# A convolution and whitening kernel: scratch in 4 KB runs, output by whole tiles, and all stores issued by ScalarE

## The chip, the core and the metric

One NeuronCore of a Trainium2 chip runs the whole program. The metric is the device time of one execution in microseconds. Besides the plain times there is one profiled execution, whose trace the rows below come from. The engines are called PE (TensorE, matrix), DVE (VectorE), ACT (ScalarE), POOL (GpSimd) and SP (SyncE, which issues DMAs).

## The reference

Input x is [4, 64, 256, 256] in float32. Layer 0 is a long convolution over both axes with a filter that is separable per channel, plus a bias term; layer 1 whitens the channels:

```python
hx, hy = implicit_filter(z, X...), implicit_filter(z, Y...)   # [256, 64] each: small MLP with sines, times a decay
k = hx[i, c] * hy[m, c]                                        # per channel c, rank one in (i, m)
y = irfft2(rfft2(x, 512) * rfft2(k, 512) / 512)[:256, :256]    # causal 2-D convolution
x = y + x * bias[:, None, None]
x1 = transpose(x, (1, 0, 2, 3)).reshape(64, -1)
x1_s = x1[:, ::9]
cov = x1_s @ x1_s.T / n + 0.01 * eye(64)                       # 64 x 64
deconv = newton_schulz_inverse_sqrt(cov, 5)
out = deconv @ (x1 - mean(x1_s))                               # back to [4, 64, 256, 256]
```

The covariance needs all of the convolved image, so the convolved values have to be kept or stored before the last product can begin.

## The kernel before, in words

**Units.** The convolution is done in 128 units. A unit is one channel of one sweep; a sweep (2 of them) covers two images. Its data are 128 partitions (the row within a half image) by 1,024 floats (image, half, column): 512 KB. Units 0 to 63 are sweep 1, 64 to 127 sweep 2.

**Per unit q.** SP loads x (`load_x`, L204, four units ahead, after `y_done` of the unit that had the slot) and the filter's Hankel block (`load_hankel`, L214, 256 KB in 1 KB runs, three buffers). ACT makes the rounded high parts of the filter, of x and of the middle result V (`flip`, `round_x`, `round_v`), POOL and DVE the low parts. PE makes V (`make_v`) and then y (`make_y`), each from Toeplitz products in three rounded terms and one plain one (L598 to L601; L601 makes two instructions). DVE adds the bias term and writes y to one of two buffers `y_sb` (`finish_y`, L477); for that it waits until the store of unit q - 2 has landed (`y_stored`). POOL masks every ninth value (L337) and DVE sums (L485) for the covariance. SP stores y to the DRAM scratch `convolved` (`store_y`, L216 to L223) in 512 runs of 1 KB, on the same queue as the loads.

**Order on the queues.** In iteration q SP issues `load_x(q + 4)`, `store_y(q - 1)`, `load_hankel(q + 5)`, `load_kept(q)`, each after its waits. ACT does `round_v(q)`, `round_x(q + 2)`, `flip(q + 2)`. PE does `make_v(q + 1)`, `make_y(q)`.

**Kept tiles.** The second product runs over 64 tiles of 128 partitions (channel and half) by 2,048 floats, 1 MB each, in rows of 8 KB. The first 14 are loaded back from the scratch during sweep 2 (`load_kept`, L230 to L239, from unit 68 on one quarter of a tile in each unit: 56 DMAs of 256 KB); seven more go to buffers that come free at the end of the convolution (L269 to L279).

**Between.** After the last unit come the covariance (L630), the Newton-Schulz iterations (small products and DVE steps, L656 to L673), about 664 to 702 us. DVE finishes the last y in two halves (L509), which wait for `y_stored` of unit 125.

**Tile phase.** For each of 64 tiles PE multiplies by the 128 x 128 matrix (L687); ACT evicts one half (L409) and DVE the other (L578) to one of four output buffers, whose earlier store must have landed. SP loads tile t + 21 when PE is done with tile t, then waits for ACT and DVE (L286, L287) and issues the stores of tile t: two DMAs of 64 partitions, 512 KB each, rows of 8 KB straight into the output's layout (L260 to L265).

Of the kernel before, what the change touches and what calls it, by code (L numbers as in the profile page):

```python
# [43 lines left out]
ZW = 2 * C + 1  # L44
X_SLOTS, T_SLOTS, H_SLOTS = 5, 3, 3

TROWS = 8
TW = TROWS * S
TILES = B * (P // TROWS)
KEPT = 14  # L50
PIECES = 4
O_SLOTS = 4
MASK_COLS = 288


def conv_whiten(nc, x, first, hidden, columns, bias, out):
    g_dram = nc.dram_tensor("filters", [2 * C, GLEN], F32, kind="Internal").ap()
    y_dram = nc.dram_tensor("convolved", [B * HB * C, P * S], F32, kind="Internal").ap()

    with ExitStack() as ctx:  # L60
        def sb(name, shape, dt=F32):
# [96 lines left out]
        def wait(eng, s, value):  # L158
            if value > 0:
                eng.wait_ge(s, value)  # L160
# [27 lines left out]
        @block.sync  # L188
        def _(sp):
            sp.dma_start(first_sb, first).then_inc(params_loaded, 16)  # L190
            sp.dma_start(col[:], columns).then_inc(params_loaded, 16)

            sp.wait_ge(w_zeroed, 1)
            for k in range(2):
                h = slice(k * ORDER, (k + 1) * ORDER)
                sp.dma_start(w_sb[h, :, h], hidden[h, :].rearrange("p (l n) -> p l n", l=3)
                             ).then_inc(params_loaded, 16)

            def load_x(q):
                if q >= UNITS:  # L200
                    return

                wait(sp, y_done, q - X_SLOTS + 1)
                sp.dma_start(x_sb[q % X_SLOTS], x[q]).then_inc(x_loaded[q % X_SLOTS], 16)  # L204

            def load_hankel(q):
                if q >= UNITS:
                    return
                k = q % H_SLOTS

                wait(sp, flipped, q - H_SLOTS + 1)
                wait(sp, t_lo_done, q - H_SLOTS + 1)
                src = bass.AP(tensor=g_dram.tensor, offset=(q % C) * GLEN, ap=[[1, P], [C * GLEN, 2], [1, S]])
                sp.dma_start(hankel[k], src).then_inc(hankel_loaded[k], 16)  # L214

            def store_y(q):  # L216
                if q < 0:
                    return
                k = q % 2
                wait(sp, y_done, q + 1)  # L220
                dst = bass.AP(tensor=y_dram.tensor, offset=(q // C) * BLOCKS * C * P * S + (q % C) * P * S,
                              ap=[[S, P], [C * P * S, BLOCKS], [1, S]])
                sp.dma_start(dst, y_sb[k].rearrange("p (i w) -> p i w", w=S)).then_inc(y_stored[k], 16)  # L223

            def tile_in(t, lo, hi):
                image, rows = t // (P // TROWS), t % (P // TROWS)
                return bass.AP(tensor=y_dram.tensor, offset=image * HB * C * P * S + rows * TW + lo,
                               ap=[[P * S, HB * C], [1, hi - lo]])

            def load_kept(q):  # L230
                n = q - (C + 4)
                if not 0 <= n < KEPT * PIECES:
                    return
                w = TW // PIECES
                lo = n % PIECES * w

                for k in range(2):
                    sp.wait_ge(y_stored[k], 16 * (C // 2))
                sp.dma_start(kept[:, n * w:(n + 1) * w], tile_in(n // PIECES, lo, lo + w)).then_inc(kept_loaded, 16)  # L239

            for q in range(4):
                load_x(q)
            sp.dma_start(bias_sb[:], bias.to_broadcast([P, C])).then_inc(bias_loaded, 16)

            sp.wait_ge(filt_ready, 1)
            sp.dma_start(g_dram, filt).then_inc(filt_stored, 16)
            sp.wait_ge(filt_stored, 16)
            for q in range(5):
                load_hankel(q)

            for q in range(UNITS):
                load_x(q + 4)
                store_y(q - 1)
                load_hankel(q + 5)
                load_kept(q)

            def load_tile(t):
                sp.dma_start(t_in[t % slots], tile_in(t, 0, TW)).then_inc(t_loaded[t % slots], 16)

            def store_tile(t):  # L260
                image, rows, k = t // (P // TROWS), t % (P // TROWS), t % O_SLOTS
                for h in range(HB):
                    dst = bass.AP(tensor=out.tensor, offset=image * C * S * S + h * P * S + rows * TW,
                                  ap=[[S * S, C], [1, TW]])
                    sp.dma_start(dst, t_out[k][h * C:(h + 1) * C, :]).then_inc(t_stored[k], 16)  # L265


            sp.wait_ge(y_mm, UNITS)
            for t in range(KEPT, after_v):  # L269
                load_tile(t)  # L270
            store_y(LAST)
            for t in range(after_v, after_y):
                load_tile(t)
            for k in range(2):
                sp.wait_ge(y_stored[k], 16 * (UNITS // 2))
            sp.wait_ge(masked_done, LAST)
            sp.wait_ge(z_last_done, PER)
            for t in range(after_y, slots):
                load_tile(t)  # L279

            for t in range(TILES):
                if t + slots < TILES:
                    sp.wait_ge(t_mm[1], t + 1)
                    load_tile(t + slots)

                sp.wait_ge(t_act, t + 1)  # L286
                sp.wait_ge(t_dve, t + 1)  # L287
                store_tile(t)
            for k in range(O_SLOTS):
                sp.wait_ge(t_stored[k], 16 * HB * (TILES // O_SLOTS))  # L290

        @block.gpsimd
        def _(pool):
# [57 lines left out]
        @block.scalar  # L351
        def _(act):
            def flip(q):
                if q >= UNITS:
                    return
                k, h = q % T_SLOTS, q % H_SLOTS
                act.wait_ge(hankel_loaded[h], 16 * (q // H_SLOTS + 1))

                wait(act, y_mm, q - T_SLOTS + 1)
                nc.scalar.copy(t_f32[k], hankel[h][:, :, :P - 1:-1])  # L360
                nc.scalar.copy(t_hi[k], hankel[h][:, :, ::-1]).then_inc(flipped, 1)  # L361

            def round_x(q):
                if q >= UNITS:
                    return
                k = q % X_SLOTS
                act.wait_ge(x_loaded[k], 16 * (q // X_SLOTS + 1))

                wait(act, v_mm, q - 1)
                nc.scalar.copy(x_hi[q % 2], row_block(k, 0)).then_inc(x_hi_done, 1)  # L370

            def round_v(q):
                k = q % 2
                wait(act, v_mm, q + 1)

                wait(act, y_mm, q - 1)
                nc.scalar.copy(v_f32[k], ps_v[k][:, :, S:2 * S])  # L377

                nc.scalar.copy(v_hi[k], ps_v[k][:, :, 0:S]).then_inc(v_hi_done, 1)  # L379

            act.wait_ge(rate_ready, 1)
            nc.scalar.activation(decay, pos, ACT.Exp, scale=rate[:]).then_inc(decay_ready, 1)
            round_x(0)
            for layer in range(3):
                act.wait_ge(f_dve, layer + 1)
                nc.scalar.activation(hid, arg, ACT.Sin).then_inc(f_sin, 1)
            round_x(1)
            flip(0)
            flip(1)

            for q in range(UNITS):
                round_v(q)
                round_x(q + 2)
                flip(q + 2)

            act.wait_ge(filt_zeroed, 2)
            nc.scalar.activation(small[:, 7:8], small[:, 7:8], ACT.Sqrt)
            act.wait_ge(n_mm, 1)
            nc.scalar.activation(small[:, 1:2], ps[:, 0, 0:1], ACT.Sqrt).then_inc(n_act, 1)
            act.wait_ge(n_act, 1)  # L400
            nc.scalar.activation(small[:, 3:4], small[:, 1:2], ACT.Sqrt).then_inc(n_act, 1)
            act.wait_ge(d_ready, 1)

            for t in range(TILES):
                act.wait_ge(t_mm[0], t + 1)

                wait(act, t_stored[t % O_SLOTS], 16 * HB * (t // O_SLOTS))
                src = ps[:, bank(t, 0):bank(t, 0) + 2, :].rearrange("p r n -> p (r n)")
                nc.scalar.activation(t_out[t % O_SLOTS][:, 0:TW // 2], src, ACT.Identity,  # L409
                                     bias=small[:, 6:7]).then_inc(t_act, 1)  # L410

        @block.vector
        def _(dve):
# [159 lines left out]
            for t in range(TILES):  # L573
                dve.wait_ge(t_mm[1], t + 1)

                wait(dve, t_stored[t % O_SLOTS], 16 * HB * (t // O_SLOTS))
                src = ps[:, bank(t, 1):bank(t, 1) + 2, :].rearrange("p r n -> p (r n)")
                nc.vector.tensor_scalar(t_out[t % O_SLOTS][:, TW // 2:TW], src, small[:, 6:7], None, ALU.add  # L578
                                        ).then_inc(t_dve, 1)
# [139 lines left out]
```

## Time and profile before

| | us |
|---|---|
| runs of the kernel: median (lowest, highest), 3 runs | 998.5 (994.86, 1002.09) |
| the profiled execution, its own time | 994.94 |
| its span from the first to the last instruction | 993.1 |
| PE busy (matmul) | 881.0 (89%) |
| DVE busy | 574.7 (58%) |
| POOL busy | 496.4 (50%) |
| ACT busy | 397.8 (40%) |
| all DMA, moved | 303.39 MB, mean 306 GB/s |

Busy times are sums over the span, and a busy PE is not a PE at its peak, since matmuls are pipelined. The DMA share is the mean busy share of the core's 16 DMA engines. The convolution takes the span's slices up to about 664 us, the tile phase those from about 702 us.

### The profile page before, as it was taken

How to read it: one execution, taken by the hardware profiler on the slowest of the kernel's cores; microseconds unless marked ns; L12 is line 12 of the kernel's file. 1: busy time of each engine (PE TensorE's matmuls, PEld its weight loads, DVE VectorE, ACT ScalarE, POOL GpSimd, SP SyncE). 2: the span in 40 equal slices, each digit the busy share in tenths (PEclk: the TensorE clock that was granted, in tenths of full speed). 3: DMA queues.
4: the chain of work that ended last, by engine and by line, in shares of the span. 5: the costliest groups of instructions: out<-in, count | busy, mean ns of one | idle time of the engine just before them, and what ended most of it. 6: DMA issues, size and time to landing. Idle time of an engine off the chain costs nothing.

```text
span 993.1 us, 15420 instructions
## 1 busy us (share of the span) xinstructions
PE 881.0 (89%) x5904; PEld 731.0 (74%) x5904; DVE 574.7 (58%) x642; ACT 397.8 (40%) x714; POOL 496.4 (50%) x277
## 2 busy tenths in 40 slices
PE   1799999999999999999999999977997777777896
PEld 0799999999999999999989899976432222222342
DVE  4487788778787657677767676771222222222332
ACT  2455555555555435454444444420121222222332
POOL 2488888889898747777767677760000000000000
PEclk9999999999999999999999999997799999999999
DMA  3799999999999959999999999975499999999999
GB/s 100 161 286 272 275 309 270 268 296 287 282 292 272 298 154 312 320 304 315 309 312 300 296 298 317 312 264 214 142 425 425 427 426 425 426 427 426 362 326 287
DMA packets 147301, 303.39 MB, mean 306 GB/s; under 512 B 10619, under 2 KB 109084, under 8 KB 132636
## 3 DMA queue, kind: packets, MB, share of 16 engines
q1 hardware_dynamic: 147228, 302.41, 92.1%
q8 instruction: 47, 0.77, 0.3%
q14 instruction: 26, 0.21, 0.1%
HBM read 167.96 MB, written 134.41 MB: 304 GB/s over the span
## 4 chain that ended last, share of the span: by engine, by line
PE 47%; DMA 41%; DVE 8%; SPq 2%; issue 1%; ACT 1%; POOL 0%; DVEq 0%; ACTq 0%
DMA convolved<-y_all 24%; DMA out<-z_all 14%; PE ps L601 12%; PE ps L687 10%; PE ps L598 7%; PE ps L599 7%; PE ps L600 7%; DVE y_all L477 4%; PE ps L630 3%; DMA out<-masked_all 2%; DVE z_all L578 1%; SPq L204 1%; ACT z_all L409 1%; DMA plain<-filters 0%; SPq L265 0%
## 5 line engine op out<-in xcount | busy, mean ns | idle before, releaser
L598 PE MATMUL ps<-rounded 128*128 128x256 f32 x1024 | 373.9, 365 | 24.6 <-issue 15.3
L337 POOL TENSOR_TENSOR masked_all<-y_all,mask 128x1024 f32<-128x1024 f32 x127 | 328.8, 2589 | 80.0 <-DVE y_all L477 79.7
L599 PE MATMUL ps<-rounded 128*128 128x256 f32 x1024 | 288.3, 282 | 0.0
L600 PE MATMUL ps<-rounded 128*128 128x256 f32 x1024 | 288.3, 282 | 0.0
L477 DVE SCALAR_TENSOR_TENSOR y_all<-x_all,bias_sb,ps 128x1024 f32<-128x1024 f32 x127 | 162.5, 1280 | 139.9 <-DMA convolved<-y_all 131.7
L598 PEld LDWEIGHTS ps<-rounded 128*128 128x128 f32 x1024 | 197.3, 193 | 30.7 <-issue 30.1
L308 POOL TENSOR_TENSOR rounded<-x_all,rounded 128x512 fp32r<-128x512 f32 x128 | 165.2, 1290 | 88.6 <-ACT rounded L370 87.4
L601 PE MATMUL ps<-plain,x_all 128*128 128x128 f32 x1024 | 197.9, 275 | 0.0
L599 PEld LDWEIGHTS ps<-rounded 128*128 128x128 f32 x1024 | 197.5, 193 | 0.0
L601 PE MATMUL ps<-plain 128*128 128x128 f32 x1024 | 196.7, 274 | 0.0
L600 PEld LDWEIGHTS ps<-rounded 128*128 128x128 f32 x1024 | 193.3, 189 | 0.0
L687 PE MATMUL ps<-kept,z_all 128*128 128x512 f32 x344 | 158.6, 612 | 33.3 <-ACT z_all L409 23.8
L601 PEld LDWEIGHTS ps<-plain,x_all 128*128 128x128 f32 x1024 | 158.2, 191 | 0.0
L687 PEld LDWEIGHTS ps<-kept,z_all 128*128 128x128 f32 x344 | 64.7, 194 | 126.3 <-issue 126.0
L601 PEld LDWEIGHTS ps<-plain 128*128 128x128 f32 x1024 | 157.3, 190 | 0.0
L370 ACT CAST rounded<-x_all 128x512 fp32r<-128x512 f32 x128 | 79.7, 622 | 193.0 <-DMA x_all<-x 193.0
L485 DVE TENSOR_REDUCE z_all<-masked_all 128x116 f32<-128x1044 f32 x127 | 156.7, 1234 | 0.0
L578 DVE TENSOR_SCALAR z_all<-ps,small 128x1024 f32<-128x1024 f32 x48 | 61.6, 1284 | 152.4 <-PE ps L687 94.5
L409 ACT ACTIVATE z_all<-ps,small 128x1024 f32<-128x1024 f32 x48 | 53.5, 1115 | 173.6 <-DMA out<-z_all 124.8
L377 ACT COPY plain<-ps 128x512 f32<-128x512 f32 x128 | 74.8, 584 | 105.5 <-PE ps L601 105.1
L466 DVE TENSOR_TENSOR rounded<-plain,rounded 128x512 fp32r<-128x512 f32 x128 | 93.2, 728 | 8.1 <-ACT rounded L361 8.1
L457 DVE TENSOR_TENSOR rounded<-ps,rounded 128x512 fp32r<-128x512 f32 x128 | 87.2, 681 | 14.0 <-ACT rounded L379 13.9
(98 smaller groups left out, 471.4 us busy)
## 6 DMA issues: line engine op xcount, KB each, us to landing
x_all<-x SPq DMA_DIRECT2D x128, 512.0 KB, 6.9
convolved<-y_all SPq DMA_DIRECT2D x128, 512.0 KB, 8.0
out<-z_all SPq DMA_DIRECT2D x96, 512.0 KB, 12.7
plain<-filters SPq DMA_DIRECT2D x128, 256.0 KB, 9.1
kept<-convolved SPq DMA_DIRECT2D x29, 1024.0 KB, 18.9
out<-masked_all SPq DMA_DIRECT2D x32, 512.0 KB, 12.8
kept<-convolved SPq DMA_DIRECT2D x56, 256.0 KB, 9.5
rounded<-convolved SPq DMA_DIRECT2D x9, 1024.0 KB, 18.8
```

Source lines behind the costliest of these rows:

```text
L308: nc.gpsimd.tensor_tensor(x_lo[k], row_block(q % X_SLOTS, 0), x_hi[k].bitcast(F32), ALU.subtract).then_inc(x_lo_done, 1)
L337: nc.gpsimd.tensor_tensor(masked_of(k, 0, PER), by_image(y_sb[k]), mask_of(q // C, 0, PER), ALU.mult).then_inc(masked_done, 1)
L370: nc.scalar.copy(x_hi[q % 2], row_block(k, 0)).then_inc(x_hi_done, 1)
L457: nc.vector.tensor_tensor(v_lo[k], ps_v[k][:, :, 0:S], v_hi[k].bitcast(F32), ALU.subtract).then_inc(v_lo_done, 1)
L466: nc.vector.tensor_tensor(t_lo[k], hankel[h][:, :, ::-1], t_hi[k].bitcast(F32), ALU.subtract).then_inc(t_lo_done, 1)
L477: nc.vector.scalar_tensor_tensor(y_sb[k], x_sb[q % X_SLOTS], bias_sb[:, q % C:q % C + 1], ps_y[k].rearrange("p a n -> p (a n)"), ALU.mult, ...
L485: nc.vector.tensor_reduce(z_of(q % C), grouped(q % 2, 0, BLOCKS), AX_X, ALU.add).then_inc(z_done, 1)
L598: mm(wide, hi[:, b, cols], t_hi[k][:, f, :], start=True, stop=False)
L599: mm(wide, hi[:, b, cols], t_lo[k][:, f, :], start=False, stop=False)
L600: mm(wide, lo[:, b, cols], t_hi[k][:, f, :], start=False, stop=False)
L601: last = mm(o[:, b, m * S + P:(m + 1) * S], block1[:, b, cols], t_f32[k][:, f, :], start=False, stop=True)
L687: last = mm(ps[:, bank(t, u) + r, :], dmat, t_in[k][:, w:w + IMG], start=True, stop=True)
```

## The change

The scratch gets the layout [sweep x 128, 64 rows x 1,024]: partition (half of the rows, channel), then the row, then image, half and column. A unit's y is stored as 2 x 64 runs of 1,024 floats (4 KB). A tile is now two rows of that layout, still 128 partitions by 2,048 floats, and the kept tiles are loaded in halves, one in every second unit. The output is a tensor of 64 whole tiles, each stored by one DMA of 1 MB; the host puts the axes in order. ACT issues the stores of y (at the end of its iteration, after `flip`) and of the output tiles (after its own half and a wait for DVE's); SP only loads.

```diff
-TROWS = 8
-TW = TROWS * S
-TILES = B * (P // TROWS)
+ROWS = P // 2
+TROWS = 2
+TW = TROWS * XW
+SWEEP_TILES = ROWS // TROWS
+TILES = SWEEPS * SWEEP_TILES
 KEPT = 14
-PIECES = 4
+PIECES = 2
...
-    y_dram = nc.dram_tensor("convolved", [B * HB * C, P * S], F32, kind="Internal").ap()
+    y_dram = nc.dram_tensor("convolved", [SWEEPS * P, ROWS * XW], F32, kind="Internal").ap()
...
-            def store_y(q):
...
-                wait(sp, y_done, q + 1)
-                dst = bass.AP(tensor=y_dram.tensor, offset=(q // C) * BLOCKS * C * P * S + (q % C) * P * S,
-                              ap=[[S, P], [C * P * S, BLOCKS], [1, S]])
-                sp.dma_start(dst, y_sb[k].rearrange("p (i w) -> p i w", w=S)).then_inc(y_stored[k], 16)
...
             def tile_in(t, lo, hi):
-                image, rows = t // (P // TROWS), t % (P // TROWS)
-                return bass.AP(tensor=y_dram.tensor, offset=image * HB * C * P * S + rows * TW + lo,
-                               ap=[[P * S, HB * C], [1, hi - lo]])
+                sweep, rows = t // SWEEP_TILES, t % SWEEP_TILES
+                return bass.AP(tensor=y_dram.tensor, offset=sweep * P * ROWS * XW + rows * TW + lo,
+                               ap=[[ROWS * XW, P], [1, hi - lo]])
 
             def load_kept(q):
-                n = q - (C + 4)
-                if not 0 <= n < KEPT * PIECES:
+                n = (q - (C + 4)) // 2
+                if q % 2 or not 0 <= n < KEPT * PIECES:
                     return
...
             for q in range(UNITS):
                 load_x(q + 4)
-                store_y(q - 1)
                 load_hankel(q + 5)
                 load_kept(q)
...
-            def store_tile(t):
...
-                for h in range(HB):
-                    dst = bass.AP(tensor=out.tensor, offset=image * C * S * S + h * P * S + rows * TW,
-                                  ap=[[S * S, C], [1, TW]])
-                    sp.dma_start(dst, t_out[k][h * C:(h + 1) * C, :]).then_inc(t_stored[k], 16)
...
-            store_y(LAST)
+            sp.wait_ge(y_done, UNITS)
...
-            for t in range(TILES):
-                if t + slots < TILES:
-                    sp.wait_ge(t_mm[1], t + 1)
-                    load_tile(t + slots)
-
-                sp.wait_ge(t_act, t + 1)
-                sp.wait_ge(t_dve, t + 1)
-                store_tile(t)
+            for t in range(TILES - slots):
+                sp.wait_ge(t_mm[1], t + 1)
+                load_tile(t + slots)
...
+            def store_y(q):
+                if q < 0:
+                    return
+                k = q % 2
+                act.wait_ge(y_done, q + 1)
+                dst = bass.AP(tensor=y_dram.tensor, offset=((q // C) * P + q % C) * ROWS * XW,
+                              ap=[[C * ROWS * XW, 2], [XW, ROWS], [1, XW]])
+                act.dma_start(dst, y_sb[k]).then_inc(y_stored[k], 16)
+
             for q in range(UNITS):
                 round_v(q)
                 round_x(q + 2)
                 flip(q + 2)
+                store_y(q - 1)
+            store_y(LAST)
...
                 nc.scalar.activation(t_out[t % O_SLOTS][:, 0:TW // 2], src, ACT.Identity,
                                      bias=small[:, 6:7]).then_inc(t_act, 1)
+                act.wait_ge(t_act, t + 1)
+                act.wait_ge(t_dve, t + 1)
+                act.dma_start(out[t], t_out[t % O_SLOTS]).then_inc(t_stored[t % O_SLOTS], 16)
...
-    out = nc.dram_tensor("out", [B, C, S, S], F32, kind="ExternalOutput").ap()
+    out = nc.dram_tensor("out", [TILES, P, TW], F32, kind="ExternalOutput").ap()
...
+    tiles = r.results[0]["out"].reshape(SWEEPS, SWEEP_TILES, 2, C, TROWS, PER, HB, S)
+
+    return np.ascontiguousarray(tiles.transpose(0, 5, 3, 6, 2, 1, 4, 7)).reshape(B, C, S, S)
```

## Rows read from the trace of the kernel before

**Rows 1.** The page's 40 slices: PE and DMA in tenths busy, GB/s.
```profile
PE   1799999999999999999999999977997777777896
...
DMA  3799999999999959999999999975499999999999
GB/s 100 161 286 272 275 309 270 268 296 287 282 292 272 298 154 312 320 304 315 309 312 300 296 298 317 312 264 214 142 425 425 427 426 425 426 427 426 362 326 287
```

**Rows 2.** The page's chain that ended last: shares by line.
```profile
DMA convolved<-y_all 24%; DMA out<-z_all 14%; PE ps L601 12%; PE ps L687 10%; PE ps L598 7%; PE ps L599 7%; PE ps L600 7%; DVE y_all L477 4%; PE ps L630 3%; DMA out<-masked_all 2%; DVE z_all L578 1%; SPq L204 1%; ACT z_all L409 1%; DMA plain<-filters 0%; SPq L265 0%
```

**Rows 3.** The windows view: busy us (x instructions) by engine, clock, DMA share, GB/s.
```profile
core 0: us, PE busy (x) PEld busy (x) DVE busy (x) ACT busy (x) POOL busy (x), PEclk, DMA share, GB/s
125.00:175.00 50.00, 50.00 (x436) 50.00 (x436) 41.41 (x44) 27.69 (x55) 44.06 (x22) 1.00 0.98 289
425.00:475.00 50.00, 47.33 (x397) 46.10 (x396) 35.60 (x41) 24.31 (x50) 36.03 (x21) 1.00 1.00 311
655.00:702.00 47.00, 33.62 (x209) 30.33 (x210) 18.77 (x42) 2.93 (x6) 8.27 (x8) 0.76 0.53 202
760.00:900.00 140.00, 105.31 (x228) 40.90 (x227) 36.79 (x29) 32.05 (x29) 0.00 (x0) 0.99 1.01 426
```

**Rows 4.** The waits between 380 and 640 us: total us, times, longest.
```profile
ACT rounded L370 <- DMA x_all<-x: 125.2, 51, 4.6
DVE y_all L477 <- DMA convolved<-y_all: 76.3, 51, 3.3
```

**Rows 5.** The DMA view of 5 to 24 us: GB/s in 40 slices.
```profile
GB/s 172 310 311 388 431 414 414 414 414 431 307 115 103 65 4 0 0 0 0 0 0 0 0 0 0 0 0 0 0 0 0 0 0 0 0 0 0 171 243 0
```

**Rows 6.** The DMA view of 80 to 320 us: packets, and the queue's.
```profile
DMA packets 48926, 68.32 MB, mean 285 GB/s; under 512 B 2483, under 2 KB 42252, under 8 KB 48900
...
q1 hardware_dynamic: 48900, 67.96, 96.8%
```

**Rows 7.** The DMA view of 20 to 24 us: packets, and the filter store.
```profile
DMA packets 144, 0.20 MB, mean 49 GB/s; under 512 B 16, under 2 KB 144, under 8 KB 144
...
filters<-kept SPq DMA_DIRECT2D x1, 192.0 KB, 1.9
```

**Rows 8.** The DMA view, issues of the whole span: xcount, KB each, us to landing.
```profile
x_all<-x SPq DMA_DIRECT2D x128, 512.0 KB, 6.9
convolved<-y_all SPq DMA_DIRECT2D x128, 512.0 KB, 8.0
...
kept<-first SPq DMA_DIRECT2D x1, 49.5 KB
...
col<-columns SPq DMA_DIRECT2D x1, 2.0 KB
```

**Rows 9.** The page's packets of the whole span, by size.
```profile
DMA packets 147301, 303.39 MB, mean 306 GB/s; under 512 B 10619, under 2 KB 109084, under 8 KB 132636
```

**Rows 10.** The DMA view of 1.5 to 3 us.
```profile
DMA packets 188, 0.05 MB, mean 35 GB/s; under 512 B 155, under 2 KB 188, under 8 KB 188
```

**Rows 11.** The tile x_all: ns min/median/max, first and last start.
```profile
L477 DVE SCALAR_TENSOR_TENSOR y_all<-x_all,bias_sb,ps x127: 1267/1281/1284, 39.3 to 659.9; 128x1024 f32<-128x1024 f32 x127
...
L509 DVE SCALAR_TENSOR_TENSOR y_all<-x_all,bias_sb,ps x2: 739/742/746, 662.3 to 663.9; 128x512 f32<-128x512 f32 x2
```

**Rows 12.** Line 223: ns min/median/max of the issue, first and last start.
```profile
L223 SPq DMA_DIRECT2D convolved<-y_all x128: 360/434/1462, 41.0 to 665.4; - x128
```

**Rows 13.** SyncE's waits, whole span: total us, times, longest.
```profile
SPq L204 <- DVE y_all L477: 322.1, 122, 16.7
SPq L287 <- DVE z_all L578: 94.1, 43, 3.2
...
SPq L287 <- DVE masked_all L578: 31.9, 14, 3.1
```

**Rows 14.** The chain in order of time: start, us, what.
```profile
929.88 55.19 PE ps L687 x128
```

More of the change, by code:

```diff
@@ L214, in load_hankel @@
                 sp.dma_start(hankel[k], src).then_inc(hankel_loaded[k], 16)
-            def store_y(q):
-                if q < 0:
-                    return
-                k = q % 2
-                wait(sp, y_done, q + 1)
-                dst = bass.AP(tensor=y_dram.tensor, offset=(q // C) * BLOCKS * C * P * S + (q % C) * P * S,
-                              ap=[[S, P], [C * P * S, BLOCKS], [1, S]])
-                sp.dma_start(dst, y_sb[k].rearrange("p (i w) -> p i w", w=S)).then_inc(y_stored[k], 16)
             def tile_in(t, lo, hi):
-                image, rows = t // (P // TROWS), t % (P // TROWS)
-                return bass.AP(tensor=y_dram.tensor, offset=image * HB * C * P * S + rows * TW + lo,
-                               ap=[[P * S, HB * C], [1, hi - lo]])
+                sweep, rows = t // SWEEP_TILES, t % SWEEP_TILES
+                return bass.AP(tensor=y_dram.tensor, offset=sweep * P * ROWS * XW + rows * TW + lo,
+                               ap=[[ROWS * XW, P], [1, hi - lo]])
             def load_kept(q):
-                n = q - (C + 4)
-                if not 0 <= n < KEPT * PIECES:
+                n = (q - (C + 4)) // 2
+                if q % 2 or not 0 <= n < KEPT * PIECES:
                     return
@@ L258, in load_tile @@
                 sp.dma_start(t_in[t % slots], tile_in(t, 0, TW)).then_inc(t_loaded[t % slots], 16)
-            def store_tile(t):
-                image, rows, k = t // (P // TROWS), t % (P // TROWS), t % O_SLOTS
-                for h in range(HB):
-                    dst = bass.AP(tensor=out.tensor, offset=image * C * S * S + h * P * S + rows * TW,
-                                  ap=[[S * S, C], [1, TW]])
-                    sp.dma_start(dst, t_out[k][h * C:(h + 1) * C, :]).then_inc(t_stored[k], 16)
             sp.wait_ge(y_mm, UNITS)
@@ L279, in _ @@
                 load_tile(t)
-            for t in range(TILES):
-                if t + slots < TILES:
-                    sp.wait_ge(t_mm[1], t + 1)
-                    load_tile(t + slots)
-                sp.wait_ge(t_act, t + 1)
-                sp.wait_ge(t_dve, t + 1)
-                store_tile(t)
+            for t in range(TILES - slots):
+                sp.wait_ge(t_mm[1], t + 1)
+                load_tile(t + slots)
             for k in range(O_SLOTS):
-                sp.wait_ge(t_stored[k], 16 * HB * (TILES // O_SLOTS))
+                sp.wait_ge(t_stored[k], 16 * (TILES // O_SLOTS))
         @block.gpsimd
@@ L405, in _ @@
                 act.wait_ge(t_mm[0], t + 1)
-                wait(act, t_stored[t % O_SLOTS], 16 * HB * (t // O_SLOTS))
+                wait(act, t_stored[t % O_SLOTS], 16 * (t // O_SLOTS))
                 src = ps[:, bank(t, 0):bank(t, 0) + 2, :].rearrange("p r n -> p (r n)")
@@ L574, in _ @@
                 dve.wait_ge(t_mm[1], t + 1)
-                wait(dve, t_stored[t % O_SLOTS], 16 * HB * (t // O_SLOTS))
+                wait(dve, t_stored[t % O_SLOTS], 16 * (t // O_SLOTS))
                 src = ps[:, bank(t, 1):bank(t, 1) + 2, :].rearrange("p r n -> p (r n)")
@@ L714 @@
            for k, v in arrays.items()]
-    out = nc.dram_tensor("out", [B, C, S, S], F32, kind="ExternalOutput").ap()
+    out = nc.dram_tensor("out", [TILES, P, TW], F32, kind="ExternalOutput").ap()
     conv_whiten(nc, *aps, out)
     r = run_bass_kernel_spmd(nc, [arrays], core_ids=[0])
-    return r.results[0]["out"]
+    tiles = r.results[0]["out"].reshape(SWEEPS, SWEEP_TILES, 2, C, TROWS, PER, HB, S)
+    return np.ascontiguousarray(tiles.transpose(0, 5, 3, 6, 2, 1, 4, 7)).reshape(B, C, S, S)
```

## The prediction

> **What bounds the kernel now.** I read the page first [rows 1]: PE is busy for nearly the whole convolution (slices up to 655 us), the DMA engines from slice 3 on, and in the tile phase (from 702 us) the transfers stand at 426 GB/s. The chain [rows 2] gives 24% to the stores of y and 16% to the stores of the output. The stretches [rows 3] split the convolution in two. In sweep 1 PE is busy 50.00 of 50 us and issues 436 matmul instructions. Lines 598 to 601 are five instructions (L601 makes two) in each of 8 turns, 40 a unit, so a unit takes 50 x 40 / 436 = 4.59 us, and PE sets it. In sweep 2, with the loads of kept tiles added, there are 397 (PE busy 47.33): 5.04 us a unit, and the waits there [rows 4] name the store of y (76.3 us before L477) and the load of x (125.2 us before L370). So sweep 2 is bound by DMA, 0.45 us a unit over PE.
>
> What a packet costs follows from two windows. Between 5 and 24 us the early loads of x run at 414 GB/s in the steady slices [rows 5], 25.9 GB/s an engine: a 4 KB packet takes 0.158 us. Tiles of 8 KB rows move at 426 GB/s [rows 3], or 0.154 us per 4 KB. In sweep 1 the window 80:320 [rows 6] holds 48,900 packets in 96.8% of 16 engines: 3,717 engine-us. Less the 48,900 - 42,252 = 6,648 packets of 4 KB at 0.158 (1,050) that leaves 2,667 us for 42,252 smaller ones, nearly all of 1 KB: 0.063 us each. Check by sweep 2: per unit and engine 8 x 0.158 (x) + 32 x 0.063 (y) + 16 x 0.063 (hankel) + 8 x 0.08 (kept, half of a 4 KB packet) + 4 closing packets of 0.063 = 5.2 us, against 5.04. The prices hold.
>
> **Part 1, the store of y.** It moves 512 KB as before, now as 128 runs of 4 KB instead of 512 of 1 KB. Spread over 16 engines that is 8 x 0.158 = 1.26 us an engine for 2.02. But is it spread? The destination is now written with 2 (the halves of the partitions) as its outermost size, then 64 rows, then 1,024 elements; it was 128 outermost. The trace tells something of how many engines one DMA gets. Every DMA ends in one small packet per engine: the filter store, of 128 rows, is 144 packets [rows 7]. The whole span has 624 issues (16 lines of that view, from x's 128 to the one of columns, four of them in [rows 8]); with 640 small data packets (128 of columns, 384 of hidden, 128 of bias) and 16 closing ones each that would be 10,624 under 512 B. It has 10,619 [rows 9], five fewer. The window from 1.5 to 3 us shows where: 188 packets, 155 of them small, for the 33 rows of "first" and the 128 of "columns" [rows 10]. 188 - 161 = 27 = 16 + 11: the 33-row transfer ran on 11 engines, the largest divisor of its outer size up to 16. By the same rule the new store, cut along its outer dimension on both sides (2 and 128), runs on 2 engines. The trace can't tell the outer size from the number of runs (both 33 there), and that is the open point. I take the outer size, since a share has to be one stretch of the outer loop of both patterns. All other large DMAs, before and after, have 64 or 128 outermost.
>
> The Trainium skill, "DMA: Bandwidth & Descriptors", section "Why a DMA increments its semaphore by 16 and not by 1", says it outright: the count of engines is the largest up to 16 that divides the outermost non-1 size of both patterns, and on this path it is always the lowest-numbered ones. By that rule the sum below holds; by the number of runs (128, so 16 engines) it would be the first rival. The trace agrees for 33 rows (11 engines); which engines they are, no row shows.
>
> **The sum.** If it is 2 engines, and the same 2 each time, each gets 64 packets of 4 KB a store: 64 x 0.158 = 10.11 us. On them also lie their shares of the loads: x 8 x 0.158 = 1.26, hankel 16 x 0.063 = 1.01, closing packets 0.2: 12.6 us a unit, and 35 us in all for the 14 kept tiles (14 x 8 packets of 8 KB at 0.308). No engine of the core has as much: PE needs 4.59. Two buffers of y keep one store queued behind the other, so these two engines don't idle; DVE's 1.28 us per y [rows 11] lies beside the other store. The last y (units' halves, L509, now at 663.9 us [rows 11]) waits for store 125: first store issued at 41.0 us [rows 12], then 126 x 10.11 = 1,274, loads of the 123 units not yet fetched 123 x 2.27 = 279, closings 25, kept 35: 1,613 us, so 41 + 1,613 + 1.3 = 1,655 against 664: +991. The stores of units 126 and 127 (20 us) and the seven tile loads (7 x 2.46 = 17) then run beside the covariance and the iterations (664 to 702, 38 us): nothing. The profiled execution took 994.94 us (span 993.1, 1.8 outside): 994.9 + 991 = 1,986, say 1,985. The profiled execution lies 0.4% below the runs' median of 998.5, which is nothing beside this.
>
> Bounds of the store's 4 KB packet, which no row shows: below, 0.154 (the tiles' rate, and somewhat less if fourteen engines are out of the way: 0.150); above, 0.168 from the line through 1 KB (0.063) and 8 KB (0.308), and at the far end 4 x 0.063 = 0.252. With 0.150 and a hankel packet at 0.045 (a quarter of 0.154 and a little for the short run): 126 x 9.6 + 123 x 1.92 + 60 = 1,506, in all 1,880. With 0.168: 126 x 10.75 + 123 x 2.35 + 60 = 1,704, in all 2,077; a bubble of 1 us a unit on top, if a full queue holds up the next issue, 2,205. At 0.252: 126 x 16.1 + 123 x 3.0 + 60 = 2,458, in all 2,830, which I hold for unlikely since the load of x has the same runs at 0.158.
>
> **Part 2, who issues.** ACT gets 128 issues of about 0.43 us [rows 12] and waits for the y before each; behind the wait stand the rounding of V and the next flip. ACT is busy 27.7 of 50 us [rows 3], the y is ready 1.3 us after its matmuls while the flip of the same iteration takes about 1.0, and the next V is ready 2.3 us (half a unit of PE) after them: with fast stores no cost, at most 0.43 x 128 = 55 us if nothing hid it; a gain of up to 5 us isn't excluded, as SP's queue gets shorter by these issues. With slow stores ACT is held until y is done, but one unit's V is then rounded already; PE has 12.6 us for 4.59, even at half its clock (9.2), so nothing. SP's wait for y at L204 (322.1 us [rows 13]) stays; what goes is its wait at L287 (94.1 and 31.9 us), behind which the next tile load was queued.
>
> **Part 3, loads of kept tiles**, 28 of 512 KB for 56 of 256 KB: the same bytes, packets of 4 KB for 2 KB, 0. Scratch rows now lie 256 KB apart instead of 128; the output was written at that distance and the tile phase ran at 426 GB/s [rows 3]: 0, bounds -2 and +10.
>
> **Part 4, the tile phase.** 64 stores of 1 MB for 128 of half, contiguous; bytes equal. Loads are released by PE as before, PE by the four output buffers, so loads and stores keep alternating at 426 GB/s until tile 43, and the last 21 tiles go at PE's 3.45 us (16 tiles in 55.19 us [rows 14]). ACT's issue follows DVE's half (1.28 us) and ends before PE's next half: 0, bounds -8 (stores no longer behind loads) and +8. After a slow convolution PE's clock may be low for a while, as between 655 and 702 us (0.76 [rows 3]): up to +10, in the range.
>
> **The rivals.** *All 16 engines take part* (number of runs decides): the y store costs 1.26 us for 2.02, sweep 2 needs 5.2 - 0.76 = 4.4 us of DMA, below PE's 4.59, and its 57 units go from 5.04 to 4.59: -26 us, 969 us: faster. It decides at the engines of a store: with 8 a store would be 16 x 0.158 = 2.53 us on each, more than today's 2.02, so only 16 make it faster. For it: 128 runs, and 33 rows don't exclude it. Against: the only odd transfer followed its outer size. A dearer ACT or tile phase could bring this case to no change. *Two engines, but others each time*: then no engine is overfull, but a store lasts 10.1 us and shares its engines with loads, about 14.3 till it lands; with two buffers a unit takes (14.3 + 1.3 + 1.4) / 2 = 8.5 us: 64 x 3.9 + 62 x 3.46 = +464, 1,460 us. Against it: 11 of 16 in one transfer says nothing of turns, and no row speaks for them. *The change doesn't do what it says* would mean that ACT's stores still wait their turn behind SP's loads; with the larger packets that is about the first rival's time.
>
> **How the numbers follow.** Two fixed engines 0.82, all sixteen 0.15, changing engines 0.03. The two cases of two engines are slower: 0.85. Of the 0.15, 0.12 is faster by over 1% and 0.03 within 1% (1% is about what a measurement of this kernel can tell). The range is the first case's own, 1,830 to 2,240, from 1,880 and 2,205 with some 40 us each way; it leaves out the two rivals and a few hundredths at the edges, 0.2 in all.
>
> **What would show it.** The y store lands 20 us or more after its issue (8.0 now [rows 8]); DMA share in the convolution near (2 x 12.6 + 14 x 2.6) / (16 x 12.6) = 0.3 at 105 to 120 GB/s; PE busy a third or so of each stretch; the chain nearly all convolved<-y_all until 1,650 us; small packets fewer by 14 per y store. The tile phase stays at 426 GB/s and about 290 us. The forecast is wrong if the share stays at 0.9 with units of 4.6 us (first rival), or if stores land in 12 to 15 us with units of 8 (second).

## The result, and the profile after

The changed kernel takes 1,910.6 us (median of 4 runs, 1,909.2 to 1,912.3) against 997.8 before: a ratio of 1.914, 95% interval 1.907 to 1.922. Predicted were 1,985 (1,830 to 2,240), slower. The profiled execution took 1,909.2 us with a span of 1,907.3, against 994.9 and 993.1. All ratios here are of fast executions; one slow one of e6_act_issues (2,482 us) and two of e1_halves (1,006 and 1,008 us) are left out of them, and no trace shows what held them up.

The slices of the page after, under those of [rows 1], with the granted clock:

```profile
PE   4555555555555555665555555555655554977788
...
PEclk9877777777777777787777777777777776999999
DMA  4333333333333333444444444444444432899997
GB/s 130 99 111 111 110 109 111 110 110 110 111 111 110 111 111 110 111 120 130 129 127 118 130 130 128 118 119 129 130 130 127 119 134 103 339 427 427 428 426 309
```

The convolution is stretched to 33 of 40 slices (up to 1,586 us). In it PE is half busy, the DMA engines show a share of 0.3 to 0.4 where they had 0.9, and 99 to 134 GB/s flow where most slices had 264 to 320. The chain by line, against [rows 2]:

```profile
DMA convolved<-y_all 76%; DMA out<-z_all 6%; PE ps L682 5%; DVE y_all L472 4%; DMA out<-masked_all 3%; PE ps L625 1%; DVE z_all L573 0%; ACT z_all L401 0%; DVE masked_all L573 0%; PE ps L596 0%; DVE kept L432 0%; DMA plain<-filters 0%; PE ps L661 0%; PE ps L593 0%; PE ps L665 0%
```

The stores of y have 76% of the span instead of 24%. The stretches that answer to [rows 3] (sweep 1, sweep 2, tile phase):

```profile
300.00:600.00 300.00, 174.51 (x1007) 170.47 (x1006) 92.95 (x101) 61.27 (x128) 101.40 (x52) 0.78 0.37 111
...
1000.00:1300.00 300.00, 164.31 (x956) 160.40 (x955) 87.60 (x96) 56.62 (x118) 85.54 (x49) 0.77 0.43 126
1622.00:1907.00 285.00, 231.25 (x513) 94.80 (x512) 82.33 (x65) 71.32 (x64) 0.00 (x0) 0.99 0.94 394
```

The tile phase has PE's clock of 0.99 as before, and takes 285 us. In the convolution the clock averages 0.78, so PE spends part of it at the lower of its two levels, idle as it is between units. That costs nothing, since PE does not set the pace there; what is waited for is seen in the waits from 200 to 800 us:

```profile
ACT plain L358 <- DVE y_all L472: 486.8, 51, 10.7
DVE y_all L472 <- DMA convolved<-y_all: 420.6, 51, 9.4
```

DVE waits for y's store before each of the 51 units, 8.2 us on average; ACT's 487 us are the same wait one step on, since it stands at the y it has to store. How long a store is under way the chain in order of time shows (start, us). It holds every second store, one in 23.75 us, and a unit takes half of that, so two stores are under way at a time:

```profile
117.57 22.42 DMA convolved<-y_all
141.32 22.42 DMA convolved<-y_all
```

22.4 us, against a median of 8.0 from issue to landing before [rows 8]. The time per unit comes from the adds of y in sweep 1 and in sweep 2: the time between the first and the last start, divided by the count less one.

```profile
L472 DVE SCALAR_TENSOR_TENSOR y_all<-x_all,bias_sb,ps x25: 1279/1280/1283, 308.5 to 595.1; 128x1024 f32<-128x1024 f32 x25
```

```profile
L472 DVE SCALAR_TENSOR_TENSOR y_all<-x_all,bias_sb,ps x24: 1279/1280/1281, 1008.9 to 1298.1; 128x1024 f32<-128x1024 f32 x24
```

(595.1 - 308.5) / 24 = 11.94 us and (1,298.1 - 1,008.9) / 23 = 12.57 us. The same reading of the kernel before gives 5.15 us in sweep 2:

```profile
L477 DVE SCALAR_TENSOR_TENSOR y_all<-x_all,bias_sb,ps x47: 1279/1281/1284, 401.5 to 638.2; 128x1024 f32<-128x1024 f32 x47
```

That it is two engines, the packets tell, against [rows 9]:

```profile
DMA packets 91300, 303.37 MB, mean 159 GB/s; under 512 B 7355, under 2 KB 40284, under 8 KB 76636
```

Under 512 B there are 3,264 fewer: 28 kept loads and 64 output stores fewer at 16 closing packets each (1,472), and 128 stores of y at 14 fewer each (1,792). Each store of y closes with 2 packets. And what a packet of a store costs, the queues show (q10 is ACT's: packets, MB, share of 16 engines), from 200 to 800 us:

```profile
DMA packets 27383, 66.12 MB, mean 110 GB/s; under 512 B 1700, under 2 KB 14500, under 8 KB 27358
...
q1 hardware_dynamic: 20813, 39.38, 26.0%
q10 hardware_dynamic: 6545, 26.40, 10.7%
```

10.7% of 16 x 600 us is 1,027 engine-us for 6,545 packets. The trace's records of single packets have 6,445 of 4 KB among them at 0.159 us each, and 100 closing ones at 0.009. An engine's 64 are 10.2 us of the unit's 11.94; what is left for the loads is 1.7. (The expectations below were written with 0.157, the average over both kinds, and so with 10.05.)

### The profile page after: what moved, and what is told of

It reads as the page before. It is cut to its first block, busy times and chain, and to the rows that moved or that the text cites. A ratio compares the mean times of both kernels' runs of the same rounds, so it can differ in the third digit from the quotient of the medians.

```text
span 1907.3 us, 15300 instructions
## 1 busy us (share of the span) xinstructions
PE 1141.7 (60%) x5904; PEld 979.5 (51%) x5904; DVE 578.1 (30%) x642; ACT 387.1 (20%) x714; POOL 490.0 (26%) x277
## 2 busy tenths in 40 slices
DMA packets 91300, 303.37 MB, mean 159 GB/s; under 512 B 7355, under 2 KB 40284, under 8 KB 76636
## 4 chain that ended last, share of the span: by engine, by line
DMA 85%; PE 7%; DVE 6%; ACT 1%; issue 0%; SPq 0%; ACTq 0%; DVEq 0%
DMA convolved<-y_all 76%; DMA out<-z_all 6%; PE ps L682 5%; DVE y_all L472 4%; DMA out<-masked_all 3%; PE ps L625 1%; DVE z_all L573 0%; ACT z_all L401 0%; DVE masked_all L573 0%; PE ps L596 0%; DVE kept L432 0%; DMA plain<-filters 0%; PE ps L661 0%; PE ps L593 0%; PE ps L665 0%
## 5 line engine op out<-in xcount | busy, mean ns | idle before, releaser
L593 PE MATMUL ps<-rounded 128*128 128x256 f32 x1024 | 475.5, 464 | 653.8 <-issue 639.9
L593 PEld LDWEIGHTS ps<-rounded 128*128 128x128 f32 x1024 | 268.1, 262 | 674.1 <-issue 668.6
L594 PE MATMUL ps<-rounded 128*128 128x256 f32 x1024 | 355.8, 347 | 0.0
L595 PE MATMUL ps<-rounded 128*128 128x256 f32 x1024 | 353.8, 345 | 0.0
L596 PE MATMUL ps<-plain,x_all 128*128 128x128 f32 x1024 | 299.1, 392 | 0.0
L594 PEld LDWEIGHTS ps<-rounded 128*128 128x128 f32 x1024 | 270.1, 264 | 0.0
L595 PEld LDWEIGHTS ps<-rounded 128*128 128x128 f32 x1024 | 264.6, 258 | 0.0
L596 PEld LDWEIGHTS ps<-plain,x_all 128*128 128x128 f32 x1024 | 258.1, 307 | 0.0
L596 PE MATMUL ps<-plain 128*128 128x128 f32 x1024 | 206.4, 285 | 0.0
L596 PEld LDWEIGHTS ps<-plain 128*128 128x128 f32 x1024 | 170.2, 204 | 0.0
L461 DVE TENSOR_TENSOR rounded<-plain,rounded 128x512 fp32r<-128x512 f32 x128 | 87.9, 687 | 8.0 <-ACT rounded L342 8.0
```

Source lines behind the costliest of these rows:

```text
L461: nc.vector.tensor_tensor(t_lo[k], hankel[h][:, :, ::-1], t_hi[k].bitcast(F32), ALU.subtract).then_inc(t_lo_done, 1)
L593: mm(wide, hi[:, b, cols], t_hi[k][:, f, :], start=True, stop=False)
L594: mm(wide, hi[:, b, cols], t_lo[k][:, f, :], start=False, stop=False)
L595: mm(wide, lo[:, b, cols], t_hi[k][:, f, :], start=False, stop=False)
L596: last = mm(o[:, b, m * S + P:(m + 1) * S], block1[:, b, cols], t_f32[k][:, f, :], start=False, stop=True)
```

## The experiments

Two questions were open: whether it is the number of engines and nothing else in the change, and what the rest of the change is worth. The last part of the second led to a third, what binds sweep 2. All ratios are to the kernel before, on the same chip.

**Undo the outer size alone (e1_halves)**

```diff
-                dst = bass.AP(..., ap=[[C * ROWS * XW, 2], [XW, ROWS], [1, XW]])
-                act.dma_start(dst, y_sb[k]).then_inc(y_stored[k], 16)
+                for h in range(2):
+                    dst = bass.AP(..., ap=[[XW, ROWS], [1, XW]])   # offset: + h * C rows of the scratch
+                    act.dma_start(dst, y_sb[k][h * ROWS:(h + 1) * ROWS, :]).then_inc(y_stored[k], 16)
```

> The changed kernel with one edit: each store of y goes out as two DMAs of 64 partitions, so the outermost size is 64 on both sides instead of 2 and 128; layout, run length (4 KB), issuing engine and output stay. Theory A (a store with outer size 2 runs on two fixed engines): every store is spread over 16 engines, a unit of sweep 1 takes PE's 4.59 us and one of sweep 2 under 4.8, total 960 to 985 us, faster than the kernel before; y stores land in 3 to 6 us. Theory B (ACT's issue and its wait for y hold up PE): unchanged, about 1,900. Theory C (4 KB writes or the new scratch layout are dear): unchanged or at most 10% less, 1,700 to 1,900.

Measured: 996.1 us, ratio 1.004 (1.001 to 1.007). One edit, which leaves layout, run length and issuing engine alone, gives back all but some 4 of the 913 us: B and C fall. But A's own 960 to 985 was missed too: with 16 engines the change gains nothing. Its profiled execution lies 1.2% over its median, so its sizes are rough, but the group of ACT's copy after the two stores shows a new wait, and the timeline its source:

```profile
L358 ACT COPY plain<-ps 128x512 f32<-128x512 f32 x128 | 75.2, 588 | 318.3 <-issue 175.8 <-PE ps L597 142.5
```

```profile
204.28 1.11 ACTq L380 DMA_DIRECT2D convolved<-y_all  x2
205.48 0.59 ACT L358 COPY plain<-ps 128x512 f32<-128x512 f32 x1 [1.80 <-issue]
```

Two issues keep ACT for 1.1 us in every unit, and the V that it rounds next comes late. That it is ACT's time, e3_halves_sp and k16 below bear out: with the two issues on SP a unit of sweep 1 takes 4.73 us, with one issue on ACT it is at PE's pace. A unit of sweep 1 took (329.3 - 82.7) / 49 = 5.03 us:

```profile
L473 DVE SCALAR_TENSOR_TENSOR y_all<-x_all,bias_sb,ps x50: 1269/1276/1282, 82.7 to 329.3; 128x1024 f32<-128x1024 f32 x50
```

**SP issues instead: halves (e3_halves_sp) and the two-engine store (e2_two_sp).** The same two forms, in `store_y` of SP at its old place.

> As e1_halves, but SP issues the stores of y, in the place it had before (behind the load of x, ahead of the Hankel load). Theory A: about e1_halves, 960 to 985 us, the difference to it (under 10 us) being what ACT's queue is worth for y. Theory B: 960 to 985 here and about 1,900 in e1_halves. Theory C: both at 1,700 to 1,900.

> The changed kernel with only the issue of y's stores put back on SP, still as one DMA with outer size 2. Theory A: the two engines have the same work, 1,890 to 1,960 us, a unit of sweep 1 at 11.9 us or a little more. Theory B: back to 960 to 1,000. Theory C: about 1,900.

Measured: e3 990.9 us, 0.998 (0.995 to 1.002), so 5 us less than with ACT, and again not the 960 to 985 expected. e2 1,895 us (one run): with the issue back on SP some 904 of the 913 us of loss stay. This closes theory B from its other side. The adds of y of e3 in sweep 1 and sweep 2, and of e2 in sweep 1, give (328.7 - 82.7) / 52 = 4.73, (634.6 - 400.2) / 46 = 5.10 and (589.4 - 303.9) / 24 = 11.90 us a unit:

```profile
L472 DVE SCALAR_TENSOR_TENSOR y_all<-x_all,bias_sb,ps x53: 1267/1281/1283, 82.7 to 328.7; 128x1024 f32<-128x1024 f32 x53
```

```profile
L472 DVE SCALAR_TENSOR_TENSOR y_all<-x_all,bias_sb,ps x47: 1268/1280/1282, 400.2 to 634.6; 128x1024 f32<-128x1024 f32 x47
```

```profile
L471 DVE SCALAR_TENSOR_TENSOR y_all<-x_all,bias_sb,ps x25: 1279/1280/1282, 303.9 to 589.4; 128x1024 f32<-128x1024 f32 x25
```

**ACT issues, nothing else (e6_act_issues).** The kernel before with `store_y` and `store_tile` moved to ACT unchanged.

> The kernel before with one part of the change alone: ACT issues the stores of y (still 1 KB runs, outer size 128) and of the output (still two per tile), SP only loads. Theory A: DMA time per unit is unchanged, so sweep 2 stays near 5.0 us a unit: 985 to 1,000 us, same as before. Theory B: clearly slower, by some hundred us. Theory C: same as before.

Measured: 998.8 us, 1.005 (1.003 to 1.008): issuing from ACT costs 3 to 8 us here, nothing of the order of the result. It has one more use: the stores of y have a queue of their own in it, with 1 KB packets (80 to 320 us).

```profile
DMA packets 48863, 68.26 MB, mean 284 GB/s; under 512 B 2476, under 2 KB 42187, under 8 KB 48838
...
q1 hardware_dynamic: 21473, 40.74, 64.2%
q10 hardware_dynamic: 27365, 27.18, 32.0%
```

```profile
x_all<-x SPq DMA_DIRECT2D x52, 512.0 KB, 5.8
```

32.0% of 3,840 engine-us are 1,229 for 27,365 packets, nearly all of 1 KB: a 1 KB packet of y costs 0.046 us, not 0.063. So the 32 packets of a store were 1.47 us, and eight of 4 KB are 1.27: the long runs save 0.2 us a unit, not 0.76. The load queue has the other 2,465. How they divide, the records of single packets in the same window tell:

| | packets | mean, us | median, us |
|---|---|---|---|
| y's stores, 1 KB | 26,539 | 0.046 | 0.046 |
| Hankel reads, 1 KB | 13,172 | 0.071 | 0.046 |
| loads of x, 4 KB | 6,651 | 0.228 | 0.159 |
| closing packets | 2,476 | 0.009 | 0.009 |

Nine in ten Hankel packets are as short as those of y, and the rest take longer, some of them many times as long. The loads of x have such a tail as well. (The expectations of k8 and e8 below take the Hankel packets at about 0.1 us; they got that by putting every packet of x at 0.158.)

**The count of engines as the only knob (k4, k8, k16)**

```diff
-                              ap=[[C * ROWS * XW, 2], [XW, ROWS], [1, XW]])
+                              ap=[[GROUP, P // GROUP_ROWS], [XW, GROUP_ROWS], [1, XW]])
```

`GROUP_ROWS` is 32, 16 or 8 and `GROUP` one row longer than the rows in it; for this the scratch is ordered by channel and then half, and a tile is loaded in two halves.

> The changed kernel with the scratch rows of a unit laid out so that its one store has outermost size 4 (groups of 32 rows with a pad of one row between them; runs stay 4 KB, ACT issues). The tiles are loaded in two halves of 64 partitions. Theory A (engines = outermost size, the same ones each time): 32 packets of 0.157 us = 5.0 us a store on each of four engines, plus the 1.8 us of loads that the changed kernel showed there (11.87 less 10.05), 6.85 us a unit and 7.5 in sweep 2: 1,230 to 1,310 us in all. Theory D (the engines change from store to store): no engine is overfull and PE sets the pace, 980 to 1,030 us. Closing packets: 4 per store.

> As k4 with groups of 16 rows, outermost size 8. Theory A: 16 x 0.157 = 2.5 us a store plus 1.8 (2.4) us of loads, 4.35 us a unit in sweep 1, below PE's 4.59, and 4.95 in sweep 2: 980 to 1,020 us. If the Hankel packets cost 0.1 us each on a busy engine, as their share of queue time suggests, it is 5.4 and 6.0 us a unit: 1,050 to 1,110 us. Theory D: as k4, 980 to 1,030.

> As k4 with groups of 8 rows, outermost size 16: one DMA a store on all 16 engines, issued by ACT in one go (about 0.5 us) where e1_halves needed two (1.1 us). If ACT's issue time is what keeps e1_halves at 5.04 us a unit in sweep 1, PE sets the pace again here (4.59 to 4.65) and the time is 970 to 990 us. If the 4 KB runs themselves are as dear as the 1 KB runs, sweep 2 stays near 5.0 and the time is 985 to 1,000.

Measured: 1,300 us and 1,063 us (one run each), and 1,002.3 us, 1.014 (1.008 to 1.020). The adds of y of k4 and of k8 in sweep 1:

```profile
L479 DVE SCALAR_TENSOR_TENSOR y_all<-x_all,bias_sb,ps x60: 1279/1280/1282, 79.7 to 494.0; 128x1024 f32<-128x1024 f32 x60
```

```profile
L479 DVE SCALAR_TENSOR_TENSOR y_all<-x_all,bias_sb,ps x50: 1279/1280/1283, 82.6 to 327.5; 128x1024 f32<-128x1024 f32 x50
```

| outermost size | us a unit, sweep 1 | the store's packets on an engine, at 0.159 us | rest | whole kernel, us |
|---|---|---|---|---|
| 2 (changed kernel) | 11.94 | 10.2 | 1.7 | 1,911 |
| 4 | 7.02 | 5.1 | 1.9 | 1,300 |
| 8 | 5.00 | 2.5 | 2.5 | 1,063 |
| 16 | PE's 4.6 | 1.3 | | 1,002 |

The pace follows the number of packets on an engine, and k4's closing packets follow too: the changed kernel's 7,355 packets under 512 B, 256 for two more a store, 1,248 for 50 tile loads in halves and 28 more kept loads, are 8,859.

```profile
DMA packets 92804, 303.38 MB, mean 234 GB/s; under 512 B 8859, under 2 KB 41788, under 8 KB 78140
```

Theory D would have had k4 at 980 to 1,030 us. The time of k8 lies in the branch with dear Hankel packets, but its 5.00 us a unit in sweep 1 lies between the 4.35 and the 5.4 of the two branches. k16 missed both of its branches: it is 1.4% slower than the kernel before. A single issue of ACT is back at PE's pace in sweep 1, which e1_halves was not, but sweep 2 takes (639.2 - 400.3) / 46 = 5.19 us, no less than before, and the tile phase 290.5 us (998.2 less 707.7), 5.5 more than in the changed kernel, whose tiles are not loaded in halves:

```profile
225.00:275.00 50.00, 50.00 (x434) 50.00 (x433) 40.09 (x44) 26.90 (x53) 43.43 (x22) 1.00 0.97 281
```

```profile
L479 DVE SCALAR_TENSOR_TENSOR y_all<-x_all,bias_sb,ps x47: 1264/1279/1282, 400.3 to 639.2; 128x1024 f32<-128x1024 f32 x47
```

**Whole tiles alone (e7_tiles_out).** The kernel before; `sp.dma_start(out[t], t_out[t % O_SLOTS])` in place of two DMAs of 64 partitions.

> The kernel before with one part alone: the output as 64 whole tiles, each stored by one DMA of 1 MB and 128 partitions, still issued by SP. Theory E (the shorter tile phase of all runs with whole tiles, 284 to 285.5 us against 291.5 before and 293.4 with ACT issuing halves, is due to the whole-tile store): 984 to 989 us, 6 us less than the kernel before. Otherwise: same as before within 2 us.

Measured: 986.0 us, 0.995 (0.993 to 0.997), as expected. The first tile's product starts at 698.3 us and the span ends at 983.9: 285.6 us against 291.5 before. Of the parts of the change this one is worth having.

```profile
L683 PE MATMUL ps<-kept,z_all x344: 592/592/1219, 698.3 to 977.5; 128*128 128x512 f32 x172
```

**What binds sweep 2 (e8_hankel_aligned, e9_hankel_65).** Both on the kernel before; what changes is which filter values are read, so what is convolved is not the reference's filter.

```diff
-                src = bass.AP(tensor=g_dram.tensor, offset=(q % C) * GLEN, ap=[[1, P], [C * GLEN, 2], [1, S]])
+                src = bass.AP(tensor=g_dram.tensor, offset=(q % C) * 64, ap=[[64, P], [C * GLEN, 2], [1, S]])   # e9: 65
```

> The kernel before with one edit: the 128 source rows of each Hankel load lie 256 bytes apart in DRAM instead of 4 bytes (so the filter block is not the right one; sizes, counts and runs of 1 KB stay). Theory F (the Hankel reads, not the stores of y, are the dear packets: about 0.1 us each by the load queue's share when the stores have their own queue, against 0.045 for the 1 KB stores, because their rows start at odd addresses or overlap): sweep 2 falls from 5.0 us a unit toward PE's 4.59 and the time to 970 to 980 us, and the Hankel load lands a microsecond or more earlier. Theory G (what binds sweep 2 is the landing time of y's store with two buffers, whatever the packets): 988 to 995 us, same as before.

> As e8_hankel_aligned (966 us), but the source rows lie 65 elements (260 bytes) apart: spread out over 33 KB as there, and starting at odd addresses as in the kernel before. If the place is what costs (all 128 rows within 1.5 KB of DRAM, read by 16 engines at once), it stays at 963 to 970 us; if the odd start of the rows costs, it goes back to 985 to 995.

Measured: 966.0 us, 0.965 (0.958 to 0.971), and 965.9 us, 0.969 (0.967 to 0.971). The Hankel load's row of the DMA view from 380 to 560 us (count, KB, median us to landing), before, in e8 and in e9, and e8's stretch in sweep 2:

```profile
plain<-filters SPq DMA_DIRECT2D x35, 256.0 KB, 9.6
```

```profile
plain<-filters SPq DMA_DIRECT2D x39, 256.0 KB, 6.5
```

```profile
plain<-filters SPq DMA_DIRECT2D x39, 256.0 KB, 6.5
```

```profile
425.00:475.00 50.00, 50.00 (x436) 50.00 (x435) 40.25 (x44) 26.97 (x55) 39.60 (x23) 1.00 1.01 346
```

With the same packets, bytes and queue, the load lands 3.1 us earlier and PE is full in sweep 2 (436 instructions in 50 us, 397 before [rows 3]); e8 came out 4 us below the range expected. Odd starts don't matter; that a filter's 128 rows lie within 1.5 KB does. The records of single packets from 380 to 560 us show where: the 1 KB packets (stores and Hankel reads together) average 0.046 us in e8 and in e9 for 0.055 before, so their tail is gone, and the 2 KB reads of kept tiles 0.084 for 0.100. The loads of x keep theirs (0.216 and 0.218, 0.208 before). Theory G falls: no buffer was added, and DVE's wait for y's store between 380 and 560 us, before and in e8, went from 52.8 us to 0.6:

```profile
DVE y_all L477 <- DMA convolved<-y_all: 52.8, 35, 3.3
```

```profile
DVE y_all L477 <- DMA convolved<-y_all: 0.6, 1, 0.6
```

**A version that beats both (e10_copies).** e7, and the filters 16 times over in DRAM, each copy read by one group of 8 rows. One further DMA writes the other 15 copies after the first three Hankel loads, which read the first copy alone. The load of the later units:

```diff
+                for f in range(2):
+                    at = (f * C + q % C) * COPIES * GLEN
+                    src = bass.AP(tensor=g_dram.tensor, offset=at, ap=[[GLEN + 8, COPIES], [1, 8], [1, S]])
+                    sp.dma_start(hankel[k][:, f, :], src).then_inc(hankel_loaded[k], 16)
```

> A version meant to beat both, computing all of it: e7_tiles_out (whole-tile output on SP, 1 KB scratch runs in one DMA with 128 outermost), and the filters kept in DRAM in 16 copies, so that the 16 groups of 8 rows of a Hankel load read 16 different places (two DMAs a unit, one per filter; the copies are written once, 2.9 MB, behind the first loads). If the crowding of all rows in 1.5 KB is what costs, sweep 2 is at PE's 4.6 us a unit and the time is 960 to 968 us: 966 less the 5 us of the tile phase, plus some 2 to 6 us for writing the copies at the start. If 16 places within 24 KB don't relieve it, or the extra issue on SP costs what it gives, 980 to 990.

Measured: 963.2 us, 0.971 (0.968 to 0.973), 29 us under the kernel before, about 5 of them e7's. Sweep 2 runs at PE's pace:

```profile
425.00:475.00 50.00, 50.00 (x436) 50.00 (x435) 40.67 (x45) 27.67 (x55) 40.08 (x23) 1.00 1.03 343
```

## Why the prediction was right

**Two engines a store, the same ones.** Right: 2 closing packets a store, and k4, k8 and k16 show that it is the outermost size that decides, all with 128 runs. That they are the same each time follows from the pace (changing pairs were priced at 8.5 us a unit, and with changing engines k4 was expected at PE's pace, and it took 7.02), not from a row that names them. The Trainium skill, "DMA: Bandwidth & Descriptors", section "Why a DMA increments its semaphore by 16 and not by 1", has the count as the largest up to 16 that divides the outermost sizes of both patterns. The closing packets of the traces agree at 2, 4, 8, 11 and 16.

**The sum.** +991 was forecast for the convolution's end; L504 starts at 1,586.3 us where L509 did at 663.9: +922. First store and last y:

```profile
L379 ACTq DMA_DIRECT2D convolved<-y_all x128: 486/500/1074, 39.5 to 1587.8; - x128
...
L504 DVE SCALAR_TENSOR_TENSOR y_all<-x_all,bias_sb,ps x2: 746/746/747, 1584.8 to 1586.3; 128x512 f32<-128x512 f32 x2
```

From 39.5 to 1,586.3 us are 1,547, of 1,613 forecast. The stores' term was good: 126 x 10.2 = 1,285 for 1,274. The mis-sized term is the loads and closing packets on the two engines, 279 + 25 + 35 = 339 forecast, 262 left over as measured: 1.7 us a unit of sweep 1 rather than 2.5. Part of it is plain from the packet records of 200 to 800 us: a closing packet took 0.009 us and was priced at 0.063, and the median Hankel packet took 0.046, so a unit's loads come to 8 x 0.159 + 16 x 0.046 = 2.0. The rest stays open. Over all 16 engines the load packets averaged more than that (x 0.219, Hankel 0.084, together 3.1 us a unit and engine), so those on the two engines are either cheaper than the average or their recorded times lie over the store's; the records name no engine. After the convolution: 36.0 us from there to the tile phase for 37.7, and 285.0 for 291.5 in it (-8 together; 0 was forecast, bound -8). 922 - 8 = 914, the difference of the spans.

**The parts priced at nothing.** ACT's queue: right as to the result, 5 us by e6. Lower clock on PE: right that it costs nothing. But PE was busy 0.55 to 0.58 of the convolution's stretches and not "a third or so", as its matmuls took longer at the lower clock (L593's average 464 ns, 365 for the same line before). Kept pieces and the new pitch: no run parts them, but the tile loads at the new pitch kept 427 GB/s. Tile phase: its gain was missed, and e7 puts it on the whole-tile store.

**The first rival was wrong in its time.** 969 us for 16 engines never came: 996, 991 and 1,002 did. The step that failed is the price of 0.063 us for every small packet. It was what remained after each packet of x had been put at 0.158, and in that window those averaged 0.230. The 1 KB packets averaged 0.054, a mixture of y's stores (0.046 in e6) and dearer Hankel reads (0.071). The check by sweep 2 couldn't find that, since both sweeps have about the same mix. With 0.046 the rival saves 0.2 us a unit instead of 0.76, and sweep 2 stays bound by its loads: 5.10 us a unit in e3 and 5.19 in k16, for 5.15 before. So "only 16 make it faster" was wrong too.

## What to carry to other kernels

Before a DMA's access pattern is rewritten, look at the outermost count on both sides: it sets how many engines carry it, and the closing packets in the trace give the number. Longer runs are worth nothing while the number of engines falls, and here little even when it doesn't. A price that is averaged over a queue should be split by kind of transfer before a saving is worked out from it. A queue of its own does that for one kind; what is left over for the others is again an average, and single packet records part it.

## What the runs showed of the hardware

- Where 16 engines read 128 overlapping rows out of 1.5 KB of DRAM, some of the 1 KB packets take far longer than the others: they averaged 0.071 us at a median of 0.046 (e6). With the rows spread over 33 KB (e8, e9) that tail is gone, and a unit of sweep 2 falls from 5.15 to 4.6 us, as it does with 16 copies within 24 KB (e10). What in the memory is crowded, the runs don't tell.
- A DMA share of 0.97 to 1.0 did not mean that no more could pass: at the same share sweep 2 moved 311 GB/s before and 346 with the rows spread. The share adds up the packets' recorded times, and packets of one size differ much in it: half of x's 4 KB packets took 0.159 us or less and their average was 0.208 to 0.230.
- Every DMA closes with one small packet per engine that carries it, of 0.009 us here, so the count of packets under 512 B tells how many engines a store had: 2, 4, 8 or 16.
- The two engines of a store moved it at 4,096 B / 0.159 us = 26 GB/s each, about the rate that each has when all 16 work (426 / 16 = 26.6).
- A tile stored as one DMA over 128 partitions instead of two over 64 shortened the tile phase by 6 us in 292 at the same bytes. Why was not tried.
